# When TensorE transposes the score maxima: behind one group of scores, or behind two groups and the latents' scores

## The reference, cut to what matters

```python
h = layernorm(x) * (1 + ca) + sa
x = x + ga * attention(h, ...)
h = layernorm(x) * (1 + cb) + sb
x = x + gb * ffn(h, ...)
```

```python
scores = where(allowed, einsum(q, k) * scale, NEG)
attn   = softmax(scores)                  # local, 16 heads, window of 128
local  = einsum(attn, v)
lattn  = softmax(where(lat_allowed, einsum(rq, rk) * lscale, NEG))
remote = einsum(lattn, rv) @ rout_w + rout_b
mixed  = gate * local + (1 - gate) * remote
out    = mixed @ out_w + out_b
```

## Time and profile before

| what | us |
|---|---|
| median of 3 runs | 575.29 |
| lowest and highest of them | 574.83, 580.44 |
| the profiled execution's own time | 574.33 |
| its span (first to last instruction) | 572.6 |
| TensorE (PE) busy in the span | 487.8 (85%) |
| VectorE (DVE) busy | 436.1 (76%) |
| GpSimd (POOL) busy | 379.1 (66%) |
| ScalarE (ACT) busy | 348.5 (61%) |

### The profile page before, as it was taken

The page is one execution under the profiler, slowest core; times in us unless marked ns, Lnnn a source line. Parts: engine busy times, 40 slices in busy tenths (PEclk is TensorE's granted clock), DMA queues, the critical chain, the costliest instruction groups (busy, mean ns, idle before and its releaser), DMA issues.

```text
span 572.6 us, 19855 instructions
## 1 busy us (share of the span) xinstructions
PE 487.8 (85%) x7168; PEld 367.4 (64%) x7168; DVE 436.1 (76%) x1193; ACT 348.5 (61%) x868; POOL 379.1 (66%) x516
## 2 busy tenths in 40 slices
PE   2535879899799989999999899999999899988661
PEld 2304557677577767777777677677777677766441
DVE  2156645988589978888889888888899688877554
ACT  1211465677577756677677667777777676666530
POOL 2222345777578758877788688777787587756663
PEclk9977889999899989999999999999999899989875
DMA  9558743707444453426171717171625344440000
GB/s 277 116 138 249 172 99 63 160 30 190 71 94 94 95 93 76 95 67 110 49 137 39 151 38 144 37 148 39 134 56 118 69 99 90 94 67 10 11 10 19
DMA packets 56523, 55.15 MB, mean 96 GB/s; under 512 B 7380, under 2 KB 53100, under 8 KB 54892
## 3 DMA queue, kind: packets, MB, share of 16 engines
q1 hardware_dynamic: 53564, 52.57, 41.4%
q10 hardware_dynamic: 2864, 1.31, 1.1%
HBM read 37.07 MB, written 16.80 MB: 94 GB/s over the span
## 4 chain that ended last, share of the span: by engine, by line
PE 64%; issue 13%; POOL 9%; DVE 6%; ACT 4%; DMA 2%; ACTq 1%; SPq 1%; POOLq 0%; DVEq 0%
PE p_pv L818 8%; PE p_qkv L730 8%; PE p_qkv L740 6%; PE p_misc L884 5%; PE p_y L805 4%; PE p_x L785 4%; PE p_y L806 4%; PE p_x L778 4%; PE p_a L751 3%; POOL pr L441 2%; PE p_a L830 2%; PE p_misc L867 2%; PE p_qkv L858 2%; PE p_a L716 2%; POOL pr L445 2%
## 5 line engine op out<-in xcount | busy, mean ns | idle before, releaser
L592 ACT ACTIVATE pr<-p_y 128x512 f32<-128x512 f32 x224 | 122.5, 595 | 56.7 <-PE p_y L806 55.9
L1158 DVE TENSOR_REDUCE mtok<-p_x 128x3 bf16<-128x480 f32 (+1 forms) x192 | 109.3, 585 | 30.5 <-PE p_x L785 28.8
L441 POOL TENSOR_SCALAR_AFFINE_SELECT pr<-pr 128x512 f32<-128x512 f32 x128 | 89.5, 700 | 10.7 <-ACT pr L594 6.8
L451 POOL TENSOR_TENSOR rstd<-ve,half 128x1 f32<-128x1 f32 x96 | 58.3, 607 | 47.9 <-DVE ve L1078 47.7
L469 POOL TENSOR_TENSOR dif<-local,rem 128x272 f32<-128x272 f32 x32 | 30.9, 966 | 81.7 <-DVE local L1196 81.7
L445 POOL TENSOR_SCALAR_AFFINE_SELECT pr<-pr 128x512 f32<-128x512 f32 x112 | 81.9, 732 | 0.0
L806 PE MATMUL p_y<-qst,kst 112*128 112x128 bf16 x512 | 73.1, 220 | 1.0 <-ACT qst L583 1.0
L805 PE MATMUL p_y<-qst,kst 112*128 112x128 bf16 x448 | 67.1, 222 | 7.4 <-ACT pr L592 4.8
L818 PE MATMUL p_pv<-pr,vp 128*18 128x128 f32 x1920 | 67.5, 281 | 2.4 <-issue 1.1
L730 PE MATMUL p_qkv<-hT,wqk 128*128 128x256 f32 x256 | 66.1, 403 | 2.2 <-DVE qkf L1110 1.3
L583 ACT ACTIVATE qst<-p_pv 16x2048 bf16<-16x2048 bf16 x32 | 59.8, 1870 | 10.1 <-PE p_pv L794 9.6
(11 more groups left out here) (131 smaller groups left out, 1099.6 us busy)
## 6 DMA issues: line engine op xcount, KB each, us to landing
scr_q<-terms SPq DMA_DIRECT2D x16, 384.0 KB, 2.6
qst<-scr_q SPq DMA_DIRECT2D x16, 384.0 KB, 4.7
scr_k<-terms SPq DMA_DIRECT2D x16, 384.0 KB, 4.4
kst<-scr_k SPq DMA_DIRECT2D x16, 384.0 KB, 5.4
qst<-scr_q SPq DMA_DIRECT2D x16, 256.0 KB, 5.4
kst<-scr_k SPq DMA_DIRECT2D x16, 256.0 KB, 6.4
out_y<-y SPq DMA_DIRECT2D x32, 128.0 KB, 1.9
x_all<-in_x SPq DMA_DIRECT2D x3, 1024.0 KB, 8.3
```

Of the source, the lines that this page charges most:

```text
L441: ins = pool.affine_select(out=own, in_=own, compare_op=ALU.is_ge, fill=0.0, base=-1, pattern=[[0, 4], [1, P]], channel_multiplier=-1)
L592: act.activation(pr[:, 2 * i:2 * i + 2, :, :], src, ACT.Exp).then_inc(exp_done[i], 1)
L1158: dve.tensor_reduce(mtok[:, t % 2, KS + h0:KS + h1], p_x[i % 2][:, 0:(h1 - h0) * w].rearrange("p (h n) -> p h n", n=w), AX_X, ALU.max, neg ...
```

## The change

`max_t(m)` moves two steps back in TensorE's list: it now stands behind `scores(t, 0)` and `lat_scores(t)`, directly ahead of `lat_out_t(m)`. No instruction is added or taken away, no wait condition is changed, and the lists of the other engines stay as they are.

```diff
                 if S:
                     scores(t, 1)
-                if T:
-                    max_t(m)
-                if S:
                     scores(t, 0)
                     lat_scores(t)
                 if T:
+                    max_t(m)
                     lat_out_t(m)
                 if S:
                     scores(t, 3)
```

## The result

The change takes 573.29 us (median of 20 runs) against 575.33 us of the kernel before (20 runs): ratio 0.9947, 95% interval [0.9922, 0.9973]. By the ratio that is 0.0053 x 575.33 = 3.0 us less. The ratio and its interval leave out runs more than 1.5% above the fastest of their kernel, the medians hold them all. I had forecast +0.3 us, in the range 572.0 to 579.0. The size was called right (no change over 1%) and the time lies in the range, but the sign was wrong: the interval leaves out no change.

A forecast was written before the change was run, and what follows sets the result against it. TensorE carries 64% of the chain, but ScalarE's list and stack landings limit what it gains. Gains of 2.2 us against losses of 2.46 give net +0.3 on 575.29: 575.6 us, range 572.0 to 579.0.

The forecast's parts named there:

- the wait goes and turns round: Transposes (L794) stop waiting for the p_pv copy (L600), 11.7 us in all; the shift (L583) waits for them instead.
- ScalarE holds what follows: From the later shift on, ScalarE is busy until `modulated` ends at S+6.75, and that holds `project_lat`.
- The 0.57 us of TensorE: TensorE's gain per slot up to `lat_out_t` (L850), from S+2.08 to S+1.51, by losing the stall.
- `project_lat` (L751) can start ... at S+6.89: In later-half tiles whose slots start without a wait, `project_lat` moves from S+7.04 to S+6.89, gaining 0.15 us.
- the transposes' price: TensorE time the transposes take, 0.16 us in both positions; they start at S+1.35 and the shift at S+1.60.
- ScalarE's list: ScalarE's work from the start of the shift to the end of `modulated`: 5.15 us, with the 0.18 pause subtracted.
- the loss: Later shift costs slots 12, 18, 20 0.65 us each, slot 14 0.15, slot 31 0.36: 2.46 us in all.
- The step about landings: Eight stalls in odd slots precede a slot starting at its stacks' landing; what TensorE gains there it waits longer.
- Rival 1: Stalls come off in full: fourteen stalls give 7.1 us, 568.2 by the median; chance 0.10.
- Rival 2: Longer idle waits for landings drop TensorE's clock, 1.94 us a stretch; three slots falling give 581.4; chance 0.07.
- Rival 3: ScalarE's delay costs the full 0.92 us in six slots that start behind a wait: +3.7, so 579.0; chance 0.15.
- L751 waits for L561 in most full-clock slots: Sign of being right: `project_lat` waits for `modulated` in most full-clock slots, where it did 2 times.

The follow-up runs named there:

- the loads first: SyncE issues even slots' query loads ahead of the store of y: on the kernel before 563.40 us (0.9801), on the change 556.21 us (0.9723).
- the change's second profile: The changed kernel measured and profiled once more, against the kernel before: 572.73 us, ratio 0.9966.
- the kernel with odd slots: Against the kernel before, transposes moved behind group 0 and the latents' scores in odd slots only: 571.44 us, ratio 0.9924.
- the early store: On top of the change, part2 ahead of the copy of p_pv on ScalarE and part3 ahead of rstd1 on GpSimd: 568.85 us, ratio 0.9892.

## Why the prediction was wrong in sign, point by point

**Right: the wait goes and turns round.** The wait of L794 for L600 is gone except in the last slot, and the shift now waits for the transposes.

**Right: ScalarE holds what follows.** The 0.57 us of TensorE came through in full nowhere. In slot 15 TensorE's own list would have brought `project_lat` to S+6.25 (an estimate: `lat_out_t` at S+1.29, and 292.57 - 287.61 = 4.96 us from there as in the earlier trace rows); it came at S+6.62, 0.14 behind `modulated`. Not all of that is the wait for `modulated`: the first transposed scores already follow the end of the shift. Slots 8, 16, 24 gained next to nothing (0.08 to 0.09), early tiles 0.07 to 0.16 with the loads first, slots 28 and 30 0.27 and 0.5, as forecast.

**The step that failed: "`project_lat` (L751) can start ... at S+6.89 ... Gain 0.15 us instead of 0.57."** It starts at S+6.62. Two terms of that sum were mis-sized. First the transposes' price, which I took as 0.16 us in both places. In the old place they cost 0.28: group 0 starts 0.57 behind S with them ahead of it (359.13 to 359.70) and 0.29 without (281.97 to 282.26). So they can start at S+1.24 and not at S+1.35, and the shift at S+1.49 and not at S+1.60: 0.11. In the new place, between the float32 matmuls of `lat_scores` and `lat_out_t`, they cost 0.05 (283.21 to 283.26), which brings `lat_out_t` forward but not the shift. Second ScalarE's list: I took the 0.18 idle off 5.33 and got 5.15. It takes 4.99. In slot 15 before, the two exponentials ahead of `modulated` took 1.12 us:

```profile
290.15 1.12 ACT L592 ACTIVATE pr<-p_y 128x512 f32<-128x512 f32 x2
```

After, they took 1.07, and `modulated` starts 0.11 before they end (287.64 against 286.68 + 1.07). Without the pause the two instructions overlap by that much, so the idle time hid more than its own length. Together 0.27 us, and the gain at that point is 0.42 instead of 0.15.

**The same two terms sized the loss.** Slots 18 and 20 lose 0.30 and 0.35 instead of 0.65, and slot 31 0.25 instead of 0.36. Slot 4, for which I had put nothing, is 0.34 shorter (15.09 to 14.74). Slot 12 I had put at a loss of 0.65: it takes 14.64 in the late order, and 14.37 in the one early profile without its stall inside group 1, so a loss of 0.27. Slot 14 I had put at a loss of 0.15: it loses 0.48 (15.57 us, and 15.58 in the change's second profile, where before had 15.09). That is neither of the two terms: its stall inside group 0 now delays the shift.

**The step about landings was too hard.** "What TensorE gains there it waits longer" is true of the odd slot. The even slot behind it then starts with ScalarE's copy done and loses its stall, if it transposes early; the kernel with odd slots shows 0.33 to 0.69 us in slots 8, 16, 24 and 28, though its profile as a whole is no shorter up to slot 28. In the change itself slots 8, 16 and 24 transpose late and keep 0.08, so this step doesn't carry its gain.

**The sum with the measured terms.** Slots 15, 21, 22, 23 at 0.44 instead of 0.15 (4 x 0.29 = 1.16), slot 4 0.34, slots 18 and 20 0.35 + 0.30 = 0.65 less lost, slot 12 0.38, slot 31 0.11: 2.6 us together, and 0.33 more lost in slot 14 leaves 2.3. The forecast of +0.3 becomes -2.0, beside -2.0 by the medians and -3.0 by the ratio. This is an estimate, and I don't claim it slot by slot: in the change the gain of slots 15, 21 and 23 shows only in kernels without the floor. In single profiles the key loads of a pair land 14.4 to 16.1 us behind S (those of slots 3 and 5 later), and one slot or another falls to a lower clock (2, 6, 10, 26, 29 before; 1, 10, 26, 29 after), each by itself as much as the effect. From slot 4 to 28 it is 363.9 us in the profile before, 365.1 after and 361.6 in the change's second profile: the first profile of the change does not show the gain there.

**The rivals.** Rival 1 (the stalls come off in full) has the wrong mechanism, but where nothing waits for a landing its size was nearer than mine: 0.43 of 0.57 per slot, and with the loads first 7.2 us between the medians, part of it clock. The Trainium skill, page "Perfetto Trace Analysis", section "Optimization Strategy", has one look for gaps on the engine to be optimised and make what ends them come sooner. Here 10.9 us of gaps went and 3.0 us came: two other bounds stood close behind, ScalarE's list and the landing. Rival 2 (longer waits cost clock) did not show: slots 18 and 28 ran at 1.00 behind waits of 1.50 and 1.51 us, slot 6 even behind 2.78, and fewer slots, not more, were at a lower clock. The length of the wait alone doesn't decide it: in the kernel with the late order from slot 28 on, slot 18 ran at 0.89 behind 1.58. Rival 3 (ScalarE's delay costs more) fell: it costs half of what I counted. Of my signs, "L751 waits for L561 in most full-clock slots" came out as 4 waits: TensorE was already held at the shift's end (26 waits of L805's weight load), so it and ScalarE arrive at `project_lat` nearly together, within the 0.14 lag, and no idle time is named.

**Open.** How the 3.0 us divide over the slots, and how much of the odd half's gain is the use of the waits; where the rest of the early store's 6 us came from; why slots 2, 6, 10 and 26 so often run at a lower clock.

## What to carry to other kernels

When a stall is removed, price what binds next as it will run, without its own pauses: ScalarE's instructions that followed without a pause overlapped here (by 0.11 us), so durations read beside a pause were too long, and a move that looks worth nothing can be worth three quarters of the stall. Ask which way round a slot starts: behind a wait the other engine's work is already done, and the old order is better there. And look for a floor such as a transfer chain before tuning an order: moving three loads ahead of one store gave 2.0% by itself, more than the change, and let the change show more.

## What was not expected of the hardware

- A transpose in bfloat16 cost TensorE 0.28 us between two groups of bfloat16 scores (group 0 starts 0.57 or 0.29 behind group 1) and 0.05 us between float32 matmuls (283.21 to 283.26), the same instruction with the same modelled 0.22 us.
- The landing of a store of 384 KB hung on how long before it the loads ahead of it had gone out: 4.1 us with query loads out 3.3 us before it, 5.6 us with loads out 2.5 us before it, 2.5 to 3.2 us with loads out 6.3 us before it. Issuing it 0.9 us sooner didn't bring the landing forward.
- ScalarE took 5.33 us for a list with one pause of 0.18 us, and 4.99 us for the same list without it, in four kernels.
